# Routed experts in 40 sorted tiles of 128 slots, all row scatters ahead of the first chunk

## The reference

```python
scores = jax.nn.sigmoid(xf @ gate_w.T + gate_b)
top_scores, top_idx = jax.lax.top_k(scores, TOP_K)          # 2 of 8 experts
top_scores = top_scores / (top_scores.sum(-1, keepdims=True) + 1e-06)
comb = (jax.nn.one_hot(top_idx, E, dtype=xf.dtype) * top_scores[..., None]).sum(1)
hdn = jax.nn.gelu(jnp.einsum('th,ehf->etf', xf, w1) + b1[:, None, :], approximate=False)
y = jnp.einsum('etf,efh->eth', hdn, w2) + b2[:, None, :]
routed = jnp.einsum('te,eth->th', comb, y)
shared = (jax.nn.gelu(xf @ sw1 + sb1, approximate=False) @ sw2 + sb2) * 0.1
```

## Time and profile before

| what | value |
|---|---|
| median of 3 runs | 862.85 us (862.37 to 865.46) |
| profiled execution, its own time | 867.54 us |
| its span, first to last instruction | 865.8 us |
| TensorE busy | 772.1 us (89%) |
| TensorE weight loads busy | 440.7 us (51%) |
| VectorE busy | 458.9 us (53%) |
| ScalarE busy | 334.6 us (39%) |
| GpSimd busy | 291.2 us (34%) |
| read from and written to memory | 23.71 MB and 2.16 MB |

### The profile page before, as it was taken

One profiled execution on the slowest core, in us unless ns is written; L12 is line 12 of the kernel. 1 busy time (PEld: TensorE's weight loads), 2 busy tenths in 40 slices (PEclk: granted clock), 3 DMA queues, 4 the chain that ended last, 5 costly groups with the idle time before them and its releaser, 6 DMA issues.

```text
span 865.8 us, 12588 instructions
## 1 busy us (share of the span) xinstructions
PE 772.1 (89%) x4993; PEld 440.7 (51%) x4993; DVE 458.9 (53%) x837; ACT 334.6 (39%) x507; POOL 291.2 (34%) x205
## 2 busy tenths in 40 slices
PE   5889999999889997899997989999789999978957
PEld 3333434434566465366554636556445664653533
DVE  0451304050347564769648477953765973648570
ACT  4523434433245453253534325443334452532410
POOL 0540000000002244366335445642543652443550
PEclk9799999999779997899998889999899999988986
DMA  7500000000111100000001010111000000100000
GB/s 298 238 13 13 0 0 12 0 12 0 61 61 28 41 10 14 12 14 25 17 10 38 14 26 1 25 25 37 14 5 22 14 26 13 38 14 20 7 1 13
DMA packets 22488, 26.61 MB, mean 31 GB/s; under 512 B 1291, under 2 KB 18339, under 8 KB 21796
## 3 DMA queue, kind: packets, MB, share of 16 engines
q1 hardware_dynamic: 22436, 25.88, 9.5%
HBM read 23.71 MB, written 2.16 MB: 30 GB/s over the span
## 4 chain that ended last, share of the span: by engine, by line
PE 64%; DVE 27%; issue 3%; POOL 2%; ACT 2%; DMA 1%; DVEq 0%; POOLq 0%; SPq 0%; ACTq 0%
PE ps L642 10%; PE ps L653 9%; PE ps L552 7%; PE ps L544 5%; PE ps L602 4%; PE ps L674 4%; PE ps L716 4%; PE ps L704 3%; PE ps L626 3%; PE ps L666 2%; DVE x_sb L1069 2%; PE ps L535 2%; DVE small L1085 2%; DVE l L1136 2%; PE ps L536 2%
## 5 line engine op out<-in xcount | busy, mean ns | idle before, releaser
L653 PE MATMUL ps<-work,mw 128*128 128x512 f32 x288 | 142.4, 641 | 23.0 <-DVE mtmp L1104 23.0
L892 ACT ACTIVATE work<-ps,cols 128x512 f32<-128x512 f32 x144 | 98.6, 688 | 114.1 <-PE ps L642 102.8
L642 PE MATMUL ps<-xn,mw 128*128 128x512 f32 x256 | 119.3, 610 | 0.0
L653 PEld LDWEIGHTS ps<-work,mw 128*128 128x128 f32 x288 | 58.5, 206 | 96.5 <-issue 68.3
L466 POOL TENSOR_TENSOR small<-small 128x8 f32<-128x8 f32 x32 | 54.5, 1718 | 122.7 <-DVE small L1078 122.7
L642 PEld LDWEIGHTS ps<-xn,mw 128*128 128x128 f32 x256 | 48.8, 197 | 55.4 <-issue 50.1
L1077 DVE TENSOR_REDUCE small<-sq 128x8 f32<-128x512 f32 x32 | 21.8, 680 | 90.1 <-ACT sq L880 90.1
L449 POOL CAST xb_s<-xn 128x512 fp32r<-128x512 f32 x4 | 2.4, 612 | 199.1 <-DVE xn L969 199.1
L457 POOL TENSOR_TENSOR small<-small 128x8 f32<-128x8 f32 x32 | 55.5, 1751 | 18.8 <-DVE small L1086 17.6
L704 PE MATMUL ps<-l 64*64 64x64 f32 x1024 | 36.2, 244 | 26.8 <-DVE sq L1092 26.8
L552 PE MATMUL ps<-work,l 128*128 128x512 f32 x128 | 57.4, 607 | 2.7 <-ACT work L828 2.7
(11 more groups left out here) (183 smaller groups left out, 1316.8 us busy)
## 6 DMA issues: line engine op xcount, KB each, us to landing
comb_bc<-comb_dram SPq DMA_DIRECT2D x32, 256.0 KB, 4.7
mw<-in_mw SPq DMA_DIRECT2D x1, 2304.0 KB, 8.8
l<-in_h SPq DMA_DIRECT2D x2, 1024.0 KB, 7.7
mw<-in_mw SPq DMA_DIRECT2D x1, 2048.0 KB, 17.2
x_sb<-in_xT SPq DMA_DIRECT2D x1, 1024.0 KB, 5.0
x_dram<-x_sb SPq DMA_DIRECT2D x4, 256.0 KB, 2.4
l<-x_dram SPq DMA_DIRECT2D x4, 256.0 KB, 3.3
out<-l SPq DMA_DIRECT2D x4, 256.0 KB, 2.4
```

The source lines that it names most:

```text
L642: mm = pe.matmul(to, mw1[:, e - NSPLIT, f * P:(f + 1) * P], xn[:, i * NB:(i + 1) * NB], start=True, stop=True)
L653: mm = pe.matmul(bank(7), mw2[:, e * KC + f], hid[:, e % 2, f], start=(f == 0), stop=(f == KC - 1))
L892: act.activation(hid[:, e % 2, f], take("up", i, (e, f)), ACT.Gelu, bias=col("b1", e * KC + f)).then_inc(r_act, 1)
```

## The change

The routed experts no longer run on all tokens. After the gate each token has two slots, one per chosen expert; slots are sorted by expert, each expert's rounded up to whole tiles of 128, 40 tiles in all. New in order:

- VectorE and TensorE work out each token's two slot numbers (`pos`), each tile's expert (`tile_e`) and its bias columns (`tile_tables`, in chunk 0 of block 0, after the gradients).
- TensorE turns the normalised tokens to rows, and GpSimd writes them into `xs_dram` by `pos`: 32 indirect DMAs of 128 rows (64 KB), all issued ahead of its first work of chunk 0.
- SP reads four tiles (a quad) of rows and, for each tile, the two weights of its expert (256 KB each) into one of three buffers.
- In blocks 1 and 2, five quads each: `slots_turned`, `tiles_up`, gelu, `tiles_down`, a copy and a store into `ys_dram`. Blocks 0 and 3 have none.
- In block 3 GpSimd gathers each token's two result rows (32 indirect DMAs, 8 a chunk), ScalarE multiplies by their shares, and `routed_out` adds and turns them.
- The shared expert is now the one that is split, and its down products stand in `project_out` (14 matmuls instead of 10). `mix`, `comb_bc`, their waits and the block loads from `x_dram` go.

```diff
+            def slots_in(n):
+                if n >= 2:
+                    sp.wait_ge(r_act, taken_no["qt", n - 2, 0])
+                sp.dma_start(xg[:, n % 2], xs_dram[n * 4 * P:(n + 1) * 4 * P].rearrange("(t p) d -> p t d", p=P))\
+                    .then_inc(xg_ld[n % 2], 16)
+
+            def weights_in(k):
+                if k >= 3:
+                    sp.wait_ge(d_pe, k - 2)
+                e = sp.value_load(tile_e[0:1, k:k + 1], min_val=0, max_val=EXP - 1)
+                sp.dma_start(wtile[:, k % 3, 0], a["mw1"][:, bass.ds(e, 1), :]).then_inc(w_ld[k % 3], 16)
+                sp.dma_start(wtile[:, k % 3, 1].rearrange("p (k d) -> p k d", d=D),
+                             a["mw2"].rearrange("p (e k) d -> p e k d", k=KC)[:, bass.ds(e, 1)]).then_inc(w_ld[k % 3], 16)
+
+            comb_of(0)
+            sp.wait_ge(b_bias, 1)
+            sp.wait_ge(x_st, NBLK * 16)
+            sp.dma_start(acc[:, :], x_dram).then_inc(x_ld, 16)
+            sp.wait_ge(b_tile, 1)
+            sp.wait_ge(x_sc, 2 * NT * 16)
+            slots_in(0)
...
+            def scatter_rows(count):
+                for _ in range(count):
+                    s, j = divmod(moved["out"], NT)
+                    moved["out"] += 1
+                    if s == 0 and j == 0:
+                        pool.wait_ge(z_st, 16)
+                        pool.wait_ge(b_pos, 1)
+                        pool.wait_ge(r_act, taken_no["x", 0, 3])
+                    pool.indirect_dma_start(xs_dram, bass.IndirectOffsetOnAxis(
+                        ap=pos[:, s * NT + j:s * NT + j + 1], axis=0), xtok[:, j, :], None).then_inc(x_sc, 16)
+
+            def gather_rows(count):
+                for _ in range(count):
+                    b, k = divmod(moved["in"], 8)
+                    moved["in"] += 1
+                    at = (k % 2) * NT + b * 4 + k // 2
+                    if k == 0 and b == 0:
+                        for n in range(2):
+                            pool.wait_ge(y_st[n], QUADS // 2 * 16)
+                    if k == 0 and b >= 2:
+                        pool.wait_ge(f_pe, b - 1)
+                    pool.indirect_dma_start(got[:, b % 2, k, :], None, ys_dram, bass.IndirectOffsetOnAxis(
+                        ap=pos[:, at:at + 1], axis=0)).then_inc(g_ld[b % 2], 16)
...
             split_tokens(0)
+            scatter_rows(2 * NT)
...
+            def tiles_up(n, *which):
+                for t in which:
+                    k = 4 * n + t
+                    pe.wait_ge(r_act, taken_no["qt", n, 0])
+                    pe.wait_ge(w_ld[k % 3], 32 * (k // 3 + 1))
+                    to = free("mu", n, t)
+                    for f in range(KC):
+                        mm = pe.matmul(to[:, f * P:(f + 1) * P], wtile[:, k % 3, 0, f * P:(f + 1) * P],
+                                       xgT[:, n % 2, t * P:(t + 1) * P], start=True, stop=True)
+                    mm.then_inc(r_pe, 1)
+
+            def tiles_down(n, *which):
+                for t in which:
+                    k = 4 * n + t
+                    if t == 0:
+                        bank7_free("y", n)
+                    pe.wait_ge(r_act, taken_no["mu", n, t])
+                    for f in range(KC):
+                        mm = pe.matmul(bank(7)[:, t * P:(t + 1) * P], hidt[:, k % 2, f],
+                                       wtile[:, k % 3, 1, f * P:(f + 1) * P], start=(f == 0), stop=(f == KC - 1))
+                    mm.then_inc(d_pe, 1)
...
             def project_out(i):
-                pe.wait_ge(m_mul.sem, m_mul.at(i + 1, 3) if i + 1 < NBLK else m_mul.at(i, NE))
+                bank7_free("out", i)
                 pe.wait_ge(b_cld.sem, b_cld.at(i, 16))
+                pe.wait_ge(r_act, taken_no["su", i, KC - 1])
+                pe.wait_ge(ld_m, 16)
                 pe.matmul(bank(7), wqo[:, :], xn[:, i * NB:(i + 1) * NB], start=True, stop=False)
                 pe.matmul(bank(7), mb2[:, :], combT[:, :], start=False, stop=False)
+                for f in range(KC):
+                    pe.matmul(bank(7), sw2[:, f], hid[:, f], start=False, stop=False)
...
+            def routed_out(b):
+                bank7_free("fin", b)
+                pe.wait_ge(g_sc, b + 1)
+                for k in range(8):
+                    mm = pe.matmul(bank(7)[:, k // 2 * P:(k // 2 + 1) * P], got[:, b % 2, k], mat(M_IDENT),
+                                   start=(k % 2 == 0), stop=(k % 2 == 1))
+                mm.then_inc(f_pe, 1)
...
                 turn_keys(i, 0)
                 project_targets(i, 1)
-                up(i, 0)
+                if i == 0:
+                    shared_up(0)
+                if qs:
+                    slots_turned(qs[0])
+                    tiles_up(qs[0], 0, 1)
                 if i:
                     turn_queries(i - 1, 2)
-                up(i, 1)
-                down(i, 0)
+                if qs:
+                    tiles_down(qs[0], 0)
+                    tiles_up(qs[0], 2)
+                    tiles_down(qs[0], 1)
+                    tiles_up(qs[0], 3)
+                    tiles_down(qs[0], 2, 3)
                 if i:
                     queries_through(i - 1, NCH - 1)
-                up(i, 2)
-                down(i, 1)
-                up(i, 3)
-                down(i, 2)
+                if qs:
+                    slots_turned(qs[1])
+                    tiles_up(qs[1], 0, 1)
+                    tiles_down(qs[1], 0)
+                    tiles_up(qs[1], 2)
+                    tiles_down(qs[1], 1)
+                    tiles_up(qs[1], 3)
                 updates(i, 0)
 
                 if i:
                     turn_queries(i - 1, 3)
+                if qs:
+                    tiles_down(qs[1], 2, 3)
+                keys_through(i, 1)
+                if i:
                     project_out(i - 1)
-                keys_through(i, 1)
                 project_queries(i)
                 project_targets(i, 2)
                 turn_keys(i, 1)
                 queries_through(i, 0)
-                up(i, 4)
-                down(i, 3)
                 updates(i, 1)
 
                 turn_queries(i, 0)
-                up(i, 5)
+                if i:
+                    shared_up(i)
                 keys_through(i, 2)
+                if qs:
+                    slots_turned(qs[2])
+                    tiles_up(qs[2], 0, 1)
                 queries_through(i, 1)
                 turn_keys(i, 2)
                 project_targets(i, 3)
-                down(i, 4)
-                up(i, 6)
-                down(i, 5)
-                up(i, 7)
-                down(i, 6)
+                if qs:
+                    tiles_down(qs[2], 0)
+                    tiles_up(qs[2], 2)
+                    tiles_down(qs[2], 1)
+                    tiles_up(qs[2], 3)
+                    tiles_down(qs[2], 2, 3)
+                    slots_turned(qs[3])
+                    tiles_up(qs[3], 0, 1)
+                    tiles_down(qs[3], 0)
+                    tiles_up(qs[3], 2)
+                    tiles_down(qs[3], 1)
+                    tiles_up(qs[3], 3)
+                if i == NBLK - 1:
+                    routed_out(0)
                 updates(i, 2)
```

More of the change, by code:

```diff
@@ L184, in build @@
         comb_all, combT_all = sq2[:, 0:P], sq2[:, P:2 * P]
+        mask, within, onehot1, onehot2 = (sq2[:, n * P:(n + 1) * P] for n in range(2, 6))
+        slot = within
+        table = acc[:, 0:QUADS * 4 * KC * EXP]
+        all_ones, lower = acc[:, 0:P], acc[:, P:2 * P]
+        ahead, full = acc[:, 1280:1408], acc[:, 1408:1536]
+        rows, steps, ends, tiles, bases = (acc[:, 1536 + n:1536 + n + w] for n, w in (
+            (0, 4 * QUADS), (64, NT), (80, EXP), (88, EXP), (96, EXP)))
+        expert_of, posf = acc[:, 1664:1664 + 4 * QUADS], sq2[:, 768:768 + 2 * NT]
+        matched = acc[:, 1728:1728 + 4 * QUADS * EXP]
+        share = small[:, 256:256 + 2 * NT]
+        zeros = ybuf[:, 1, 0]
         ps = ctx.enter_context(nc.psum_tensor("ps", [P, 8 * NB], F32))
@@ L634, in turn_queries, with shared_up @@
                 turn("v", i, c, lambda q: sq2[:, q * P:(q + 1) * P])
[L636 removed]
+            def shared_up(i):
                 for f in range(KC):
[L638 to L644 removed]
@@ L646, in down @@
[L646 to L655 removed]
+                    product(free("su", i, f), lambda s: sw1[:, s, f * P:(f + 1) * P],
+                            lambda s: xb_s[:, s]).then_inc(r_pe, 1)
```

454 lines of the change are left out of this document (312 added, 142 removed).

## The result

| | before | changed kernel |
|---|---|---|
| median | 862.74 us | 914.8 us |
| lowest and highest | 862.37 to 865.46 (4 runs) | 912.67 to 917.15 (4 runs) |
| ratio to before, 95% interval | | 1.0597 (1.0556 to 1.0638) |
| profiled execution; its span | 867.54; 865.8 us | 917.15; 915.3 us |
| mean granted TensorE clock | 0.92 | 0.83 |

The kernel became slower by 52 us. The prediction said slower by 18 us, 881.0, with a range up to 905. The sign was right; the size was not, and the time lies outside the range. One run of the spread scatters (927.61 us) and one of the last kernel (1015.34 us) came at a granted clock of 0.75 and 0.64 and are left out of what is said of these two kernels.

The account below looks back on a forecast made before the run. TensorE was taken to bound most of the span, VectorE's fixed chain the second chunk. Scatters' +29.4 and block 0's +4.7, with gains and losses by period, summed to +18.1: 862.85 becomes 881.0 us, range 853 to 905.

Parts of the forecast that it names:

- The scatters: Ahead of GpSimd's first powers in block 0: 32 at 1.2 us, 38.4 us, delaying the first update by 29.4.
- U(0,0): Start of the state update of block 0, chunk 0 (U(block,chunk)): forecast at 330.0 us against 300.57 before.
- the first period: Blocks 1 and 2, chunk 0's update to chunk 1's: 44 us, +5.7, with project_out ahead of queries and targets.
- The second period's chain: Blocks 1 and 2, chunk 1's update to chunk 2's: VectorE's chain 37.3 us; 38.5 taken, -3.
- U(0,3) to U(1,0): Last update of block 0 to first of block 1: 28.5 us instead of 32.8, -4.3, called chain-bound.
- with tile waits: TensorE's time in blocks 1 and 2 including weight-load waits: second period 39.4, third 33.5, fourth 29.6 us.
- the first period of block 0: Chunk 0's update to chunk 1's: 29.8 becomes 34.5 us, +4.7, for tile tables and TensorE's lower clock.
- the third periods: Blocks 1 and 2, chunk 2's update to chunk 3's: 31.5 us by the chain; 32.5 taken, +1.4.
- (1): Scatters are cheap: sum reaches zero at 0.63 us each; at SP's 0.34 the time is 853.5; chance 0.18.
- (2): Scatters are dear, 1.75 us each: +17.6, 898.6 us; chance 0.10.
- (3): Tile loads in blocks 1 and 2 are slow, 7 us instead of 4.5: 15 us more, 896; chance 0.14.
- (4): No TensorE saving in blocks 1 and 2: weight loads set 0.43 us a matmul; +34, 915 us; chance 0.06.

Follow-up runs that it names:

- the spread scatters: Changed kernel with its 32 scatters spread over the four chunks of block 0 (three, two and three a chunk): 879.72 us, ratio 1.0227.
- the last kernel: Changed kernel with scatters over three chunks, tile tables after the weight update, targets first, five weight buffers and filler matmuls: 817.98 us, ratio 0.9467.
- the tables moved: Changed kernel with VectorE making the tile tables after the first weight update instead of before it: 907.32 us, ratio 1.0507.

## Why the prediction was right in sign and wrong in size

**Right.** What bounds the kernel was read rightly: the saving on TensorE's total, 113 us, moved nothing that the chain did not let through. The scatters were the decisive term and were sized from bounds that lay a factor of five apart (0.34 and 1.75 us): taken 1.20, measured 1.26. That the guess between them came so near is in part luck, and so is U(0,0) within 0.5 us, where two errors of 2 us cancel. The place of `project_out` was named as worse than before, with 44 us for the first period; without load waits it is 44.4. The second period's chain, 37.3, is 36.5 and 36.3, the fourth's, 24.7, is 25.1. U(2,3) to U(3,0), block 3 and the end are within 1.5 us a row. Tiles go at 0.11 us a record.

**Wrong, first: the waits on tile loads, 21.6 us of the 31.4.** The step that failed is not the size of a wait but where it was counted. The prediction put "the fourth", U(0,3) to U(1,0), at 28.5, "both chain-bound", in a block that "has no routed work"; but its own rows of the order show two quads of block 1 ahead of `updates(1,0)`. There are two waits of 2.58 and 2.47 us in it, with a lower clock behind each: 34.8 instead of 28.6. The first periods were given no load wait either, and are 3.1 and 2.7 us longer by the lower clock that the waits leave behind. For the others the prediction took a value between the chain and one "with tile waits", 1.2, 1.0 and 2.8 us above the chain; measured are 3.3, 1.6 and 6.5 in block 1, 3.6 and 1.7 in block 2. Allowed for were 7.2 us in all, found 28.8. Its own values "with tile waits" would have allowed no more than 13.1: what was left out altogether, the waits ahead of U(1,0) and the first periods, is 12.

**Second: the first period of block 0, 7.0 us.** The sum has +4.7 for two things together, the tile tables and the lower clock. From U(0,0) to the targets of the second chunk it is 11.6 us before, 23.3 in the changed kernel and 17.0 with the tables moved, by TensorE's rows of these targets in the three kernels, in this order:

```profile
312.21 1.52 PE L602 MATMUL ps<-wt,xb_s 128*128 128x512 f32 x6
353.80 1.53 PE L706 MATMUL ps<-wt,xb_s 128*128 128x512 f32 x6
345.57 1.53 PE L706 MATMUL ps<-wt,xb_s 128*128 128x512 f32 x6
```

Behind the targets it is 18.2 us to U(0,1) in all three. So the tables cost 6.3 us, and the lower clock with what else changed 5.4. The term "about 5.5 us" for the tables was worked out from steps of 0.29 and 0.68 us and counted nothing for GpSimd's four additions beside them; there they are 9.4 us, of which the update covers a part, and with the tables moved 6.6 (332.49 to 339.09). The clock shows in rows such as

```profile
346.34 7.62 PE L706 MATMUL ps<-xb_s,wq 128*128 128x512 f32 x24
```

against 6.02 us for the same 24 records in block 1 (at 488.81).

**Third: the third periods, 6 us.** 31.5 by the chain were forecast, and without any load wait they are 34.4. In the kernel with five buffers the keys after U(1,2) start 10.85 us behind it:

```profile
536.80 2.80 PE L834 MATMUL ps<-l 64*64 64x64 f32 x64 [3.21 <-DVE sq L1358]
...
547.65 1.17 PE L796 MATMUL ps<-esum_s,neg 128*128 128x512 f32 x4
```

Before, from 660.51, it is 5.8 us (to 666.32). Two down tiles, a turned quad and two up tiles stand ahead of the keys, where one expert's four products stood. That is the same fault of placing that the prediction named in the first period; here its sum missed it, by 2.9 us in each block. That this order is the cause was read from the trace and not tried by itself.

These three are 21.6, 7.0 and 5.8 us. The small rows (second, first and fourth periods, U(2,3) to U(3,0), block 3, the start) make -3.0, and 31.4 is the sum.

**Readings and sums that do not come out.** 64 records in 29.6 us are 3.70 us for four matmuls, not 3.43, so 64 matmuls are 59 us of the block and not 55; nothing but the +3.4 for `project_out` could lean on it, and the eight in 7.13 us give 3.6 there. In the first period 20.2 + 3.4 + 1.7 is 25.3 and not 24.9, and with five buffers 25.4 is what it takes. The formula of the Trainium skill, page "DMA: Bandwidth & Descriptors", section "Anatomy of one DMA", which the prediction held against its own tile waits, is given for DMAs that GpSimd issues, and the weights are loaded by SP's queue.

**The rivals.** (1), cheap scatters, is out: 1.26 us against a break-even of 0.63. (2), 1.75 us, too. (3), slow loads, had the right cause, waiting for tiles, and the wrong mechanism: it wanted 7 us a load, and a load takes 4.5; and it counted longer waits at three places in each of two blocks, where there are fourteen waits, two of them ahead of U(1,0). (4) gave 915 and the time is 914.8, by coincidence: a tile's rate is 0.11 us a record, the forecast's, with the loads of TensorE's weights beside it. A number that is hit says nothing of its reason.

## What to carry to other kernels

When a step is moved into a stream whose chain is fixed, list for every period what stands in TensorE's order between the freed result and the piece the chain waits for, and count the waits there. Right ahead of an update they cost here all that they were long and more, elsewhere half to two thirds, and the lower clock behind them reached into a period that had none. A load that is issued when its buffer comes free needs room for as many tiles as pass in its latency: 4.5 us at 1.8 us a tile is 2.5 tiles, three buffers leave room for one, five for three. And a block of DMA issues on an engine that also computes is priced like computation: 32 in one go held the first update back 40 us, and spread out between the engine's other work they gave 32 to 35 of these back. How many find room is a matter of the chunk: eight did, eleven did not.

## What the runs showed of the hardware that was not expected

- An indirect DMA of 128 rows keeps GpSimd busy 0.96 us, with a gap of 0.30 us to the next; in the midst of other work single ones take up to 1.53 us:

```profile
278.28 1.53 POOL L541 DMA_INDIRECT xs_dram<-wtile,pos  x1 [0.19 <-issue]
```

(the spread kernel, GpSimd's timeline).
- Small VectorE steps beside GpSimd's additions took 0.62 and 1.19 us instead of 0.18.
- Two waits of 2.58 and 2.47 us on TensorE in otherwise dense work were followed by a clock of 0.72 from 450 to 455 and of 0.66 from 465 to 475; with five buffers it was 1.00 there. It is not so behind every wait: from 540 to 550, behind one of 2.69 us, it was 1.00.
- A load of 256 KB is listed with 3.3 us from issue to landing:

```profile
wtile<-in_mw SPq DMA_DIRECT2D x80, 256.0 KB, 3.3
```

The Trainium skill, page "DMA: Bandwidth & Descriptors", section "Anatomy of one DMA", gives 2.0 us plus bytes over 436 GB/s for DMAs that GpSimd issues; carried over to these loads of SP's queue, that is an estimate of 2.6 us. The measured 3.3 decides, and with the wait for the buffer and the register load ahead of it a tile's two loads take 4.5 us.
